# First attention of a two-layer decoder: angle by four tap-shifted combined weights, fp16 high and low products, one loading block

## The reference, cut to what matters

```
q, k, v = (causal_depthwise_conv(h @ W, conv, 4 taps) for q, k, v)
theta = q[..., ::2] * inv_freq        psi = k[..., ::2] * inv_freq
alpha, beta = sigmoid(h @ Wa), sigmoid(h @ Wb)           # one per head
state_t = rotate(state_{t-1}, theta_t - theta_{t-1}) * alpha_t + beta_t * rotate(v_t, psi_t)
out_t = rotate(state_t, -theta_t)
o = out * rsqrt(mean(out^2 over the head) + 1e-5) * rms_w * silu(h @ Wg)
x = x + o @ Wo
```

## Time and profile before

| | us |
|---|---|
| median of three timed runs | 2398.49 |
| span of the profiled execution (the only time that its page gives) | 2422.0 |
| context and identity loaded and turned | 0 to 16.6 |
| first norm | 16.6 to 33.2 |
| units and output | 33.2 to 261.15 |
| second norm | 261.5 to 277.3 |

### The profile page before, as it was taken

One profiled execution on the slowest core, in us unless ns is written; L12 is line 12 of the kernel. 1 busy time (PEld: TensorE's weight loads), 2 busy tenths in 40 slices (PEclk: granted clock), 3 DMA queues, 4 the chain that ended last, 5 costly groups with the idle time before them and its releaser, 6 DMA issues. The chain is left out here.

```text
span 2422.0 us, 41105 instructions
## 1 busy us (share of the span) xinstructions
PE 1669.1 (69%) x14892; PEld 1065.2 (44%) x14892; DVE 1665.9 (69%) x2837; ACT 1290.4 (53%) x1770; POOL 1180.4 (49%) x1087
## 2 busy tenths in 40 slices
PE   6884594277499999999874566666666654288851
PEld 3332363264277777777663122222222233166630
DVE  5999587332645555555588899999999964643435
ACT  4664485022255555555422788888888861054430
POOL 0000283243224444444434688989898960154345
PEclk8987797589699999999887555555555556599985
DMA  3000222384223323233100456565555543688933
GB/s 104 1 0 0 64 65 61 93 178 114 71 66 86 80 67 81 67 84 74 53 27 0 79 107 108 107 108 107 108 106 108 106 78 75 212 193 188 172 105 112
DMA packets 506352, 219.10 MB, mean 90 GB/s; under 512 B 425229, under 2 KB 493653, under 8 KB 506197
## 3 DMA queue, kind: packets, MB, share of 16 engines
q1 hardware_dynamic: 494677, 185.54, 34.6%
q0 software_dynamic: 11520, 31.47, 5.6%
HBM read 79.93 MB, written 36.31 MB: 48 GB/s over the span
## 5 line engine op out<-in xcount | busy, mean ns | idle before, releaser
L2134 POOL CAST xnT<-xl 128x2048 bf16<-128x2048 uint8 x256 | 483.9, 1891 | 15.4
L2172 PE MATMUL psum<-e_KT,e_QT 48*128 48x512 bf16 x1024 | 264.8, 617 | 251.6 <-DVE ctxT L2205 124.8
L2205 DVE TENSOR_SCALAR_CACHE_REDUCE ctxT<-psum,e_nsq 128x1024 f32<-128x1024 f32 x256 | 314.7, 1281 | 7.9 <-PE psum L2172 6.5
L2205 DVE TENSOR_SCALAR_CACHE_REDUCE e_Smore<-psum,e_nsq 128x1024 f32<-128x1024 f32 x256 | 314.7, 1281 | 1.7 <-issue 0.4
L2223 ACT ACTIVATE xh<-ctxT,e_ebias 128x2048 uint8<-128x2048 f32 x128 | 256.2, 2002 | 53.7 <-POOL e_ebias L2141 53.7
L2223 ACT ACTIVATE xh<-e_Smore,e_ebias 128x2048 uint8<-128x2048 f32 x128 | 256.3, 2002 | 42.2 <-POOL e_ebias L2141 42.2
L1652 POOL TENSOR_TENSOR d_sq<-d_oS 128x512 f32<-128x512 f32 x60 | 90.6, 1509 | 279.3 <-ACT d_oS L1724 279.3
L120 PE MATMUL psum<-xh,d_T 128*128 128x512 f16 x768 | 219.4, 381 | 5.6 <-ACTq L1678 5.1
L2172 PEld LDWEIGHTS psum<-e_KT,e_QT 48*128 48x128 bf16 x1024 | 33.7, 107 | 381.4 <-DVE ctxT L2205 190.1
L2386 POOL DMA_INDIRECT xnT<-kept_rows,f_token x96 | 94.2, 981 | 164.9 <-DMA f_Z<-xnT 72.7
L661 POOL TENSOR_TENSOR b_bias<-b_alibi,b_neg 128x1024 f32<-128x1024 f32 x16 | 37.8, 2365 | 278.9 <-DVE b_Vbd L760 278.9
(11 more groups left out here) (387 smaller groups left out, 4092.7 us busy)
## 6 DMA issues: line engine op xcount, KB each, us to landing
kept_y<-ctxT SPq DMA_DIRECT2D x24, 512.0 KB
kept_w<-k_WS SPq DMA_DIRECT2D x17, 640.0 KB, 3.5
f_W<-kept_w SPq DMA_DIRECT2D x17, 640.0 KB, 12.0
kept_y<-c_y SPq DMA_DIRECT2D x12, 512.0 KB
d_Wn<-in_L_attn_w_qkv SPq DMA_DIRECT2D x16, 384.0 KB, 3.5
k_W<-in_L_ffn_w_routed SPq DMA_DIRECT2D x32, 176.0 KB, 3.7
kept_rows<-xnT SPq DMA_DIRECT2D x8, 512.0 KB, 3.6
xl<-xh SPq DMA_TRANSPOSE x256
```

The source lines that it names most:

```text
L2134: pool.tensor_copy(PT[:, sl, :], P8[:, sl, :, :].rearrange("p c q -> p (c q)").bitcast(U8)).then_inc(unpacked, 1)
L2172: mm = pe.matmul(m.bank[pair_banks(c + odd) + q], QT[rows, n // 2, :], KTt[rows, n % H // 2, col:col + BLK], start=True, stop=True)
L2205: dve.tensor_scalar(S32[sl][:, hf * HALF:(hf + 1) * HALF].rearrange("p (a b) -> p a b", a=2), m.psum[:, b:b + 2, :], nsq[:, n + odd:n + od ...
```

## The change

`load_inputs`, the first `layernorm` and the weight loads become one block of a new function, `first_attention`, in a stage of its own (its semaphores are cleared at its end). x comes in four pieces, ahead of the weights; the context comes last, into the memory of `xnT`. The first norm is kept as two fp16 parts, `xh` and `xl`, as the kernel's later stages do it (x·1024 rounded to fp16, and 1024 times the rest). All weights of the projections are split likewise into high and low, and a product is three fp16 matmuls for each of two chunks.

The angle no longer goes through VectorE's taps: the convolution is linear, so for each tap j the two weight matrices are combined beforehand, `AK = Wk*conv_k[j]*turns - Wq*conv_q[j]*turns`, on GpSimd and VectorE, with `turns = inv_freq/2pi`. TensorE then adds four products into one bank, each with tokens shifted by 3 - j. VectorE subtracts the nearest whole number of turns. Rotation, squares and gate use instructions over 1024 elements in place of pairs over 512. `rms_w` is multiplied into `Wo` beforehand. The units are written out eight times in place of the loops. The context is turned by TensorE and ScalarE at the start of the second norm. The core:

```diff
-def load_inputs(nc, m, x, ctx_tokens, c_ident, x_ready):
-def rotary_recurrence(nc, m, w):
+def first_attention(nc, m, w, x, ctx_tokens, c_ident):
...
+                @block.sync            # order of the loads
+                        sp.dma_start(m.ident[:, :], c_ident).then_inc(ident_in, 16)
+                        for b in range(NBLK):
+                            sp.dma_start(m.X[:, b * TPB:(b + 1) * TPB, :], ...).then_inc(x_in[b], 16)
+                        for W, src in ((Wv, w["Wv"]), (Wg, w["Wg"])): ...
+                        for n, src in enumerate((w["Wa"], w["Wb"])): ...
+                        sp.dma_start(turns, w["turns"].partition_broadcast(P)).then_inc(conv_in, 16)
+                        for n, src in enumerate((w["conv_k"], w["conv_q"])):
+                            sp.dma_start(CB[:, n, :, :].rearrange("p c k -> p (c k)"),
+                                         src.rearrange("c k -> (c k)").partition_broadcast(P)).then_inc(conv_in, 16)
+                        for W, src in ((Wk, w["Wk"]), (Wq, w["Wq"])): ...
...
+                        sp.dma_start(m.ctx_rows, ctx_tokens.rearrange("(t p) d -> p t d", p=P)).then_inc(m.ctx_in, 16)
+                @block.gpsimd
+                    pool.wait_ge(conv_in, 16 * 3)
+                    for u in range(U):
+                        pool.tensor_tensor(CF[:, u], taps(0, u), turned_taps(u), ALU.mult).then_inc(taps_k, 1)
...
+                        pool.tensor_tensor(AK[:, u], even(Wk, u), over(CF, u), ALU.mult).then_inc(mixes, 1)
+                @block.vector          # after statistics and 1/sd
+                    normed(0)
+                    normed(1)
...
+                            dve.scalar_tensor_tensor(WX[:, 1, k, 2 * n:2 * n + 2, :], pairs(W)[:, k], SPLIT,
+                                                     WX[:, 0, k, 2 * n:2 * n + 2, :], ALU.mult, ALU.subtract)
+                    low(0)
+                    low(1)
+                    normed(2)
...
+                    normed(3)
+                    low(2)
+                    dve.wait_ge(conv_in, 16 * 3)
+                    dve.wait_ge(wqk_in, 16 * 2)
+                    angle_mix(0)
+                    low(3)
+                    angle_mix(1)
+                    angle_low(0)
+                    angle_low(1)
...
+                def project_angle(k):                               # TensorE, bank 7
+                    if k:
+                        pe.wait_ge(angle, k)
+                    for j in range(TAPS - 1, -1, -1):
+                        shift = TAPS - 1 - j
...
+                        for n, (a, b, c) in enumerate([(a, b, c) for a, b in ((0, 0), (0, 1), (1, 0)) for c in range(KC)]):
+                            mm = pe.matmul(out, WA[:, a, unit, j, c, :], moving(i, b, c, shift),
+                                           start=(j == TAPS - 1 and n == 0), stop=(j == 0 and n == 5))
...
+                for k in range(UNITS):                              # TensorE
+                    if k + 1 < UNITS:
+                        project_angle(k + 1)
+                        project(k + 1, (VE, VO))
+                    if i:
+                        output(i - 1, unit)
+                    if k + 1 < UNITS:
+                        project(k + 1, range(GE, BE + 1))
+                    pe.wait_ge(squares, k + 1)
+                    if k:
+                        pe.wait_ge(logs, k)
+                    for par in range(2):
+                        mm = pe.matmul(m.bank[4][0:M, :], mean_w[:, :], sq[:, par, :], start=(par == 0), stop=(par == 1))
...
+                for k in range(UNITS):                              # ScalarE; before it evacuate(0), sines(0)
+                    if k + 1 < UNITS:
+                        evacuate(k + 1)
+                    act.wait_ge(scanned, 2 * k + 2)
+                    act.activation(sq..., o[:, unit]..., ACT.Square).then_inc(squares, 1)
+                    if k + 1 < UNITS:
+                        sines(k + 1)
+                    act.wait_ge(meansq, k + 1)
+                    act.activation(rms[:, unit, :], m.bank[4][0:M, :], ACT.Ln, bias=eps[0:M, :]).then_inc(logs, 1)
+                    act.wait_ge(logs, k + 1)
+                    act.activation(rms[:, unit, :], rms[:, unit, :], ACT.Exp, scale=-0.5).then_inc(rms_ready, 1)
...
+                def front(k):                                       # VectorE
+                    dve.tensor_scalar(whole[:, :], turned, MAGIC * TURN, MAGIC * TURN, ALU.add, ALU.subtract)
...
+                    dve.tensor_tensor(ang[:, :], turned, whole[:, :], ALU.subtract).then_inc(angle, 1)
...
+                for k in range(UNITS):                              # VectorE; before it convolve(0), front(0)
+                    rotate(k)
+                    if k + 1 < UNITS:
+                        front(k + 1)
+                        convolve(k + 1)
+                    if i:
+                        add(i - 1, unit)
+                    back(k)
...
+        def turn_context(pe):                                       # second norm, first on TensorE
+            pe.wait_ge(m.ctx_in, 16)
+            for g in range(NBLK * KC):
...
+                    last = pe.transpose(m.bank[4 + g % 4][:, j * P:(j + 1) * P],
+                                        m.ctx_rows[:, b * TPB + j, c * P:(c + 1) * P], m.ident[:, :])
+        def keep_context(act):                                      # and first on ScalarE
...
-        layernorm(nc, m, preload)
+        layernorm(nc, m, preload, tensor_first=turn_context, scalar_first=keep_context)
...
-        rotary_recurrence(nc, m, {**own, "freq": w["freq"], "mean_w": w["mean_w"]})
+        with m.stage():
+            first_attention(nc, m, {**own, "turns": w["turns"], "mean_w": w["mean_w"]}, w["x"], w["ctx_2048"], w["ident"])
```

More of the change, by code:

```diff
@@ L64, in __init__ @@
         self.apart = self.sem("apart")
+        self.ctx_in, self.ctx_turned, self.ctx_out = (self.sem(f"ctx_{n}") for n in ("in", "turned", "out"))
         self.norms = 0
@@ L121, in split_product, with layernorm @@
     return mm
-def load_inputs(nc, m, x, ctx_tokens, c_ident, x_ready):
[L126 to L162, removed]
+def layernorm(nc, m, preload, add_to_x=False, split=False, scalar_mid=None, vector_mid=None, scalar_first=None,
+              tensor_first=None):
     stats_done, moments_done, sd_done, rstd_done, xn_ready, turned, bank_free, high = m.norm_sems
@@ L289, in rotary_recurrence @@
+        pad = sb("pad", [M, U, 2, BPB, SEQ + TAPS - 1])
         tab = sb("tab", [M, U, 2, BLK])
         gs = sb("gs", [M, U, 2, BLK])
[L291 to L292 removed]
+        whole, ang, folds = (sb(n, [M, BLK]) for n in ("whole", "ang", "folds"))
         sc = sb("sc", [M, U, 2, BLK])
         v = sb("v", [M, 2, BLK])
[L295 removed]
+        u_ = sb("u", [M, 2, BLK])
         t4 = sb("t4", [M, 4, BLK])
@@ L298, in rotary_recurrence @@
         o = sb("o", [M, U, 2, BLK])
-        sq = sb("sq", [M, U, 2, BLK])
+        sq = sb("sq", [M, 2, BLK])
         rms = sb("rms", [M, U, BLK])
[L301 to L330, removed]
@@ L343, in _ @@
[L343 to L353, removed]
-                            src = pad[:, unit, n, :, j:j + SEQ]
-                            dst = out.rearrange("p (b t) -> p b t", b=BPB)
-                            if first and j == 0:
-                                ins = dve.tensor_scalar(dst, src, wt[:, j:j + 1], None, ALU.mult)
-                            else:
-                                ins = dve.scalar_tensor_tensor(dst, src, wt[:, j:j + 1], dst, ALU.mult, ALU.add)
-                        c.do(ins)
@@ L414, in add @@
-                def add(i):
-                    for half in range(2):
-                        dve.wait_ge(outp, i * 2 + half + 2)
-                        t = i * TPB + 2 * half
-                        x2 = m.X[:, ds(t, 2), :].rearrange("p t d -> p (t d)")
-                        dve.tensor_tensor(x2, m.bank[5 + half][:, :], x2, ALU.add).then_inc(added, 1)
-                def units(i, first, last):
-                    c = Chain(dve, chain_s)
-                    c.base = i * (STEPS * U) + FRONT
[L426 to L430, removed]
-                        if not (last and unit == U - 1):
-                            front(c, k + 1, (unit + 1) % U)
-                        back(c, i, k, unit)
-                    assert c.n == STEPS * U - (FRONT if last else 0), c.n
@@ new lines, in convolve @@
+                def convolve(k):
+                    unit = k % U
+                    dve.wait_ge(evac, k * NG + VO + 1)
+                    if k == 0:
+                        dve.wait_ge(prep, 3)
+                    else:
+                        dve.wait_ge(rotated, 7 * (k - 1) + 2)
+                    for j in range(TAPS):
+                        for odd in range(2):
+                            src = pad[:, unit, odd, :, j:j + SEQ]
+                            dst = v[:, odd, :].rearrange("p (b t) -> p b t", b=BPB)
```

(7 more changed lines are left out.)

468 lines of the change are left out of this document (308 added, 160 removed).

## The result

Changed kernel: 2361.75 us, median of four runs (2353.34 to 2372.74). Beside it, kernel before: 2395.35, median of four (2392.15 to 2404.59). Ratio 0.9848, 95% interval [0.9819, 0.9876]: 36 us faster by the ratio (the two medians lie 33.6 apart), against 40.7 forecast, and inside the range.

A forecast was written before the change was run, and what follows sets the result against it. TensorE's 18.0 us a unit plus its 1.9 us wait for Square was to be the new bound, in place of VectorE. Stage 42.7 less 1.0 and 1.0 gives 40.7; 2398.5 - 40.7 = 2358 us, range 2343 to 2380.

The forecast's parts named there:

- TensorE in a unit, 18.0: Attention, each of 8 units (four token blocks by two head triples): angle, groups, half an output and mean take TensorE 18.0 us.
- The wait and the period, 19.9: Attention units: TensorE's mean waits 1.9 us for ScalarE's Square, behind six evacuations; the period becomes 19.9 us.
- VectorE in a unit, 17.6: Attention units: without the angle's taps and with wider instructions, VectorE's work falls from 25.5 to 17.6 us.
- The loading block, 37.5: Loading and first norm: first normalised tile at 13.0, block ends at 37.5 us against 34.4 before, 3.1 lost.
- The collision with GpSimd: Loading block: VectorE work stretched beside GpSimd costs 5 us if half the list is stretched, else 0; taken as 2.
- The whole stage, 42.7: From loading to the attention's last add: end at 218.4 us against 261.15, 42.7 us won, with a 19.2 us tail.
- Close and second norm, 1.0 and 1.0: Behind the attention: closing the stage costs 1.0 us, the second norm behind the context's transposes and copies another 1.0.
- The clock fell once, not in every unit: Rival, chance 0.12: TensorE's clock falls in every unit, about 3.0 us each, five of them 15, giving 2373 us.
- VectorE's waits did not stretch it to a bound: Rival, chance 0.10: waits, broadcast operands and hand-overs lift VectorE's unit period to 21.5 us, giving 2369 us.
- the wait was not won back by itself: Rival, chance 0.10: hand-overs overlap, TensorE wins its wait back and loading ends at 34.5; 12 us, giving 2346.
- loading was not held up by them: Rival, chance 0.08: broadcast convolution filters land at 45 us, not 18, moving VectorE's work some 20 us; 2378 us.
- half clock: Rival, chance 0.05: the main loop's TensorE work runs at 1.2 GHz, about 118 us more, 2476 us, slower than before.

The follow-up runs named there:

- experiment 1: Changed kernel with ScalarE doing Square of a unit ahead of the next unit's Tanh pair, not behind it; 2343.75 us, ratio 0.979.
- experiment 5: Changed kernel with Sqrt's table loaded early, in the loading block and in the second norm; 2360.72 us in a single run.
- experiment 6: Changed kernel with GpSimd's four mixing products held until VectorE has rounded the low parts of Wv and Wg; 2361.41 us in a single run.
- experiment 2: Changed kernel with the angle taking only the product of high parts, 8 matmuls in place of 24; 2337.54 us, ratio 0.9758.
- experiment 4: Changed kernel with two more 512-column matmuls in front of every projection group of six; 2385.35 us, ratio 0.9931.
- experiment 3: Changed kernel with further VectorE products in each unit before the wait for Exp: two gave 2356.52 us, ratio 0.9835; six gave 2386.61 us, ratio 0.9956.
- experiment 7: Changed kernel with 30 idle matmuls (results unread) on TensorE between its last transposes and the loading block's end; 2359.14 us in a single run.
- experiment 8: Kernel of experiment 1 with the context transposed in the attention's tail, not in the second norm; 2351.68 us, ratio 0.9801.
- 9: Changed kernel with experiment 1, experiment 5 (loading block alone), experiment 8, 42 idle matmuls before projections, 14 before the last output, Wo scaled later; 2336.42 us, ratio 0.9727.

## Why the prediction was right, point by point

- *TensorE in a unit, 18.0.* Right: 18.05 where nothing else waits (experiment 1). No time of a 96-column weight load showed: matmuls stood 0.216 apart.
- *The wait and the period, 19.9.* Right: 1.63 in place of 1.9, ended by Square; period 19.9. That it is a matter of ScalarE's order alone, experiment 1 showed by removing it: the other order of ScalarE took the period to 18.05. It adds to the period because the next unit's angle is queued behind the mean.
- *VectorE in a unit, 17.6.* Right in kind, 1.1 too long: 16.45. The chain from Square to the next scan was also shorter: no table load stands before Sin now (Sin, Abs, Sin took 1.9 from 107.07, I had 3.2).
- *The loading block, 37.5.* Mis-sized: 40.64. I had taken the first tile at 13.0; it came at 14.78, 1.3 of it Sqrt's table load, which no work covers here and which my sum of the block didn't have (experiment 5 took it out). The collision with GpSimd, taken at 2, cost 3.5: 2.6 at Wg's two products and 0.9 in the first eight tiles. Moving it (experiment 6) left 2.6. The first tile's 1.8 and these 1.5 make the 3.1 us within 0.2.
- *The whole stage, 42.7.* 39.0 came. Of the 3.7 missing, 2.5 stood at the first scan's end (66.22 against 63.7), and 1.7 are the clock's one fall at 147; the units won back some tenths. The 2.5 are a balance: 3.1 of the loading block and 0.9 of a start at half rate that lasted 5.4 us where I had 3.6, less 1.4, since no table load stood before Sin. That these errors cancel in part is luck. The tail was 19.2, as said.
- *Close and second norm, 1.0 and 1.0.* 0.7 and 0.6. In the second norm the reciprocal came 0.9 late behind Sqrt's table load, and 0.2 were won back. The size is right, the reason only in part: I had the copies at 0.54 each, but the clock fell to 0.50 at 223.5, and until it rose at 226.9, within the transposes, these paced the first copies at 0.86 (the 32 took 5.35). In experiments 2 and 4 the clock stayed at 1.00 there: the same transposes took 3.69, and the reciprocal waited 0.38, as before the change.
- *Rivals.* The clock fell once, not in every unit; VectorE's waits did not stretch it to a bound; the wait was not won back by itself; the convolution filters had landed by 16.5, so loading was not held up by them; half clock stayed at the start, at 147, in the tail and in the context's transposes.

## What to carry to other kernels

When two engines come out nearly level, read which one waits for which in the new order: 1.6 us of a wait that only the order of a third engine's instructions made, times the units, came to some 10 us here. A block that is rebuilt loses its covers: ask of each table load and each GpSimd instruction what it stands beside now. Idle matmuls in front of a short burst of TensorE work paid here, twice, where they reached up to it: 2.6 in place of 4.0 to 5.1 us for the first 12 matmuls, 7.17 in place of 9.5 to 10.5 for the last output.

## What the runs showed that I had not expected

- The same wait of about 1.65 us in front of a mean sometimes lowers TensorE's clock and mostly does not: once in seven here, with two further products in experiment 3, in 5 and in 6; three times in experiment 7, twice in experiment 4, at the one such wait of experiment 8; not in experiment 2, and not at the one of 1 and of 9. Each fall costs 1.7 us. What decides is open.
- The clock column can miss a stretch at half rate altogether: in the changed kernel it showed 1.00 from 40 to 48 while matmuls of 512 columns stood 0.425 apart up to 45.7.
- VectorE beside GpSimd lost whole instructions' time, not a share: two instructions of 0.54 became 1.53 and 2.20, four of 0.34 together 3.99, while those reading PSUM kept their 1.17. In experiment 5 it was also GpSimd that waited: its first product took 2.48 (1.18 in experiment 6), while VectorE's products beside it kept 0.55.
